# Writing out the hardware loops of two expert stages, with 23 expert numbers held in registers

## The reference, cut to what matters

```python
def ffn(x, w_gate, b_gate, W1, b1, W2, b2):         # x: 2048 x 128
    probs = softmax(x @ w_gate + b_gate)            # 8 experts
    route_p, route_idx = max(probs), argmax(probs)
    h = relu(x @ W1[e] + b1[e])                     # 128 -> 512, for each expert e
    y = h @ W2[e] + b2[e]                           # 512 -> 128
    return y[route_idx] * route_p
x = x + 0.5 * ffn(layernorm(x))
x = x + attention(layernorm(x))
x = x + 0.5 * ffn(layernorm(x))
```

## Time and profile before

| | |
|---|---|
| median of 3 runs | 393.47 us (392.41 to 393.94) |
| span of the profiled execution, first to last instruction | 387.9 us |
| TensorE busy | 270.7 us, 70% of the span |
| VectorE busy | 228.1 us, 59% |
| GpSimd busy | 204.0 us, 53% |
| ScalarE busy | 135.8 us, 35% |
| mean granted TensorE clock | 0.867 of full speed |

### The profile page before, as it was taken

One profiled execution on the slowest core, in us unless ns is written; L12 is line 12 of the kernel. 1 busy time (PEld: TensorE's weight loads), 2 busy tenths in 40 slices (PEclk: granted clock), 3 DMA queues, 4 the chain that ended last, 5 costly groups with the idle time before them and its releaser, 6 DMA issues.

```text
span 387.9 us, 7595 instructions
## 1 busy us (share of the span) xinstructions
PE 270.7 (70%) x2114; PEld 199.2 (51%) x2115; DVE 228.1 (59%) x609; ACT 135.8 (35%) x319; POOL 204.0 (53%) x351
## 2 busy tenths in 40 slices
PE   0641487777943865798999999999770396777760
PEld 0540476776831433344555555554560296777760
DVE  4959344343529778756677676776628444444434
ACT  2400132222311444056667566667420032322220
POOL 2922756666535564156565565656612566666550
PEclk9999999888985769579999999999865588968995
DMA  7950111112222055575122121100200111111217
GB/s 215 417 166 0 41 36 50 42 42 41 41 73 63 2 162 167 175 224 162 54 58 69 46 70 54 55 30 1 83 27 0 28 43 47 44 41 37 46 35 216
DMA packets 34203, 31.06 MB, mean 80 GB/s; under 512 B 3265, under 2 KB 28226, under 8 KB 34178
## 3 DMA queue, kind: packets, MB, share of 16 engines
q1 hardware_dynamic: 31234, 24.72, 20.4%
q0 software_dynamic: 2944, 6.04, 6.1%
HBM read 18.09 MB, written 12.45 MB: 79 GB/s over the span
## 4 chain that ended last, share of the span: by engine, by line
PE 57%; DVE 15%; DMA 8%; SPq 6%; issue 6%; POOL 4%; ACT 2%; another core or an unknown queue 1%; DVEq 0%; POOLq 0%; ACTq 0%
PE bank L1048 13%; PE bank L1059 13%; PE bank L1159 4%; PE bank L1185 4%; SPq L350 4%; PE bank L1135 3%; DVE xn L709 3%; DVE x L856 3%; PE bank L1182 3%; PE bank L1201 2%; PE bank L1165 2%; DVE hot_lane L787 2%; DMA xs_sb<-xn_d,tok_g 2%; DMA qz<-mT 2%; PE bank L1040 2%
## 5 line engine op out<-in xcount | busy, mean ns | idle before, releaser
L636 ACT ACTIVATE pT<-bank 128x512 f32<-128x512 f32 x96 | 57.4, 599 | 41.7 <-PE bank L1159 20.7
L439 POOL DMA_INDIRECT y_d<-ys_sb,tok_s x46 | 46.7, 1014 | 39.8 <-DVE ys_sb L831 33.2
L1059 PE MATMUL bank<-experts,hT 128*128 x368 | 56.1, 301 | 15.3 <-ACT hT L573 6.7
L1048 PE MATMUL bank<-xsT,ew 128*128 128x128 f32 x368 | 57.9, 309 | 8.6 <-ACT xsT L567 7.8
L1059 PEld LDWEIGHTS bank<-experts,hT 128*128 128x128 f32 x368 | 50.6, 213 | 17.6 <-issue 17.5
L1048 PEld LDWEIGHTS bank<-xsT,ew 128*128 128x128 f32 x368 | 53.2, 222 | 10.8 <-ACT xsT L567 8.8
L433 POOL DMA_INDIRECT xs_sb<-xn_d,tok_g x46 | 45.2, 982 | 20.3 <-issue 12.5
L902 DVE TENSOR_REDUCE mh<-bank 128x2 f32<-128x512 f32 x64 | 44.0, 689 | 13.9 <-PE bank L1135 13.3
L573 ACT ACTIVATE hT<-bank,ew 128x128 f32<-128x128 f32 x92 | 29.0, 368 | 58.2 <-PE bank L1048 46.0
L813 DVE TENSOR_SCALAR hT<-bank,ew 128x128 f32<-128x128 f32 x92 | 27.9, 345 | 36.2 <-PE bank L1048 27.2
L516 POOL TENSOR_SCALAR_AFFINE_SELECT pT<-pT 128x512 f32<-128x512 f32 x64 | 40.9, 639 | 0.0
(11 more groups left out here) (125 smaller groups left out, 429.4 us busy)
## 6 DMA issues: line engine op xcount, KB each, us to landing
sp_d<-spl SPq DMA_DIRECT2D x32, 192.0 KB, 2.9
experts<-in_experts SPq DMA_DIRECT2D x8, 578.0 KB, 8.8
qz<-sp_d SPq DMA_DIRECT2D x32, 96.0 KB
ks<-sp_d SPq DMA_DIRECT2D x32, 96.0 KB
xn_d<-xn SPq DMA_DIRECT2D x8, 256.0 KB, 3.1
yg<-y_d SPq DMA_DIRECT2D x8, 256.0 KB, 3.7
x<-in_x SPq DMA_DIRECT2D x4, 256.0 KB, 4.5
out<-x SPq DMA_DIRECT2D x4, 256.0 KB, 2.4
```

The source lines that it names most:

```text
L439: pool.indirect_dma_start(y_d[:, :], bass.IndirectOffsetOnAxis(ap=tok_s[:, t:t + 1], axis=0), ys_sb[:, t % OUT, :], None).then_inc(e_st[f] ...
L636: act.activation(pT[:, u, :], bank[2 + u % 2][:, :], ACT.Exp, scale=SCALE).then_inc(a_e, 1)
L1048: mm = pe.matmul(bank[2 + 2 * (k % 2) + c // 2][:, (c % 2) * P:(c % 2 + 1) * P], ew[:, k % WRING, c * P:(c + 1) * P], xsT[:, k % 2, :], st ...
L1059: mm = pe.matmul(bank[6 + k % 2][:, 0:D], hT[:, k % 2, c, :], w2.rearrange("p a c -> p (a c)"), start=(c == 0), stop=(c == HC - 1))
```

## The change

On ScalarE, VectorE and TensorE the loop over tiles 6 to 17 goes, and all 23 tiles are written out. On VectorE and TensorE the expert numbers are no longer read tile by tile. At the head of its stage each of these two engines waits for `te` and reads all 23 numbers into 23 registers; `weights` and `output` use the registers. VectorE's wait for `te` was at the head of its stage already, TensorE's is new. GpSimd's and SyncE's lists stay as they are. The part on ScalarE is the same replacement of the loop without the registers.

```diff
             def expert_tiles(f):                      # VectorE
+                dve.wait_ge(r_te[f], 1)
+                tile_expert = [dve.value_load(te[0:1, t:t + 1], min_val=0, max_val=NE - 1) for t in range(NS)]
+
                 def weights(t, k):
-                    e = dve.value_load(te[0:1, bass.ds(t, 1)], min_val=0, max_val=NE - 1)
+                    e = tile_expert[t]
                     need(dve, e_yc[f], t - WRING + 1)
...
-                dve.wait_ge(r_te[f], 1)
                 dve.wait_ge(e_all, 16 * NE)
                 for t in range(WRING):
                     weights(t, t)
                 relu(0, 0, 0)
-                for k in range(RING):
-                    step(k, 0, k)
-                with dve.Fori(1, NS // RING) as i:
-                    for k in range(RING):
-                        step(RING * i + k, i, k)
-                for t in range(NS // RING * RING, NS):
-                    step(t, NS // RING, t % RING, do_w=t + WRING < NS, do_h=t + 1 < NS)
+                for t in range(NS):
+                    step(t, t // RING, t % RING, do_w=t + WRING < NS, do_h=t + 1 < NS)
...
             def expert_tiles(f):                      # TensorE
+                pe.wait_ge(r_te[f], 1)
+                tile_expert = [pe.value_load(te[0:1, t:t + 1], min_val=0, max_val=NE - 1) for t in range(NS)]
...
                 def output(t, k):
-                    e = pe.value_load(te[0:1, bass.ds(t, 1)], min_val=0, max_val=NE - 1)
+                    e = tile_expert[t]
...
-                for k in range(RING):
-                    step(k, 0, k)
-                with pe.Fori(1, NS // RING) as i:
-                    for k in range(RING):
-                        step(RING * i + k, i, k)
-                for t in range(NS // RING * RING, NS):
-                    step(t, NS // RING, t % RING, do_T=t + 2 < NS, do_h=t + 1 < NS)
+                for t in range(NS):
+                    step(t, t // RING, t % RING, do_T=t + 2 < NS, do_h=t + 1 < NS)
```

More of the change, by code:

```diff
@@ L584, in expert_tiles @@
                 relu(0, 0, 0)
-                for k in range(RING):
-                    step(k, k)
-                with act.Fori(1, NS // RING) as i:
-                    for k in range(RING):
-                        step(RING * i + k, k)
-                for t in range(NS // RING * RING, NS):
+                for t in range(NS):
                     step(t, t % RING, do_T=t + 2 < NS, do_h=t + 1 < NS)
```

## The result

The changed kernel takes 405.07 us (median of four runs, 401.23 to 409.69) against 393.71 us (four runs, 392.41 to 397.26) beside it: a ratio of 1.0255 with a 95% interval of 1.0155 to 1.0354. The forecast was 410.5 us, range 399 to 417. The span of the profiled execution is 399.4 us, 11.5 us above that of before, where 17 was forecast. The two stages together are 17.1 us longer in this pair of profiles, as forecast; 5 us ahead of them that have nothing to do with the change hide part of it.

A forecast was written before the change was run, and what follows sets the result against it. No engine was full; GpSimd was nearest to a bound, 50.5 us without a pause in the first stage's 61.8 us. Span 387.9 + 20.0 (reads) - 3 (steps) = 404.9 us; time 393.47 + 17.0 = 410.5 us, range 399 to 417 us.

The forecast's parts named there:

- The reads at the head: Head of both expert stages: 23 reads in a row delay the first hidden product, 20.0 us together.
- cheap reads: Rival at the stage heads: reads overlap at a 0.30 us pitch, kernel takes 396.4 us; chance 0.12.
- TensorE's head "beside VectorE's": Stage head: TensorE's 23 reads run beside VectorE's, end 1 us earlier and cost nothing; without VectorE's, nearly as much.
- GpSimd can't work ahead: GpSimd's queue at the stage head: seven gathers at most during the reads, its remaining 50 us start 10 us later.
- What comes back in the steps: Tile steps of both stages: fewer reads and no loop give 3 us back, bounds 0 and about 23 us.
- The loop's part: Loop over tiles 6 to 17: its branches and additions cost 0 to 3 us in both stages.
- The sum: Whole kernel: 387.9 + 20.0 - 3 = 404.9 us of span, 393.47 + 17.0 = 410.5 us of time.
- The runs' median stands 5.6 us above the profiled span: Whole kernel: offset between profiled span and median time, used to turn 404.9 us into 410.5 us.
- Loop edges: Rival in the tile loop: stalls on entering a pass, 8.4 us, go; 402.1 us; chance 0.12, shared with half the pauses.
- Its other half: Rival in the tile steps: quicker steps bring back half of GpSimd's pauses, 11.5 us; 402.0 us; shared chance 0.12.
- GpSimd without pauses: Rival in both stages: all 23.1 us of GpSimd's pauses come back, kernel takes 390.4 us; chance 0.06.

The follow-up runs named there:

- Experiment 4: The changed kernel with the 23 reads at the head of both engines made without the bounds check; 398.55 us, ratio 1.017 to the kernel before.
- experiment 2: The changed kernel with the 23 head reads on TensorE alone, VectorE reading ahead of each weight copy again; 405.03 us, ratio 1.034 to the kernel before.
- experiment 1: The kernel before with all 23 tiles written out, each expert number still read tile by tile; 392.28 us against 391.97 us, ratio 0.992.
- experiment 3: The changed kernel with the head reads on VectorE alone, TensorE reading in each output product again; 407.63 us, ratio 1.042 to the kernel before.
- 7: Tiles written out, no head reads, VectorE reading for tile t + 3 at its step's start; 389.23 us against 392.64 us for the kernel before.
- 9: The kernel before with tiles written out, VectorE's reads one step ahead and GpSimd's clears held back; 384.40 us against 393.37 us, ratio 0.981.
- experiment 6: The changed kernel with GpSimd's clears at the front held back until VectorE has scaled the attention weights; 404.06 us, ratio 1.038 to the kernel before.
- Experiment 8: The changed kernel with VectorE making three reads, its first three weight copies, then the other 20 reads; 404.69 us (one run).
- experiments 5: The kernel before with GpSimd's clears at the front held back until VectorE has scaled the attention weights; 388.21 us against 392.64 us, ratio 0.994.

## Why the prediction was right, step by step

**The reads at the head** are right in kind and size. Forecast were 0.62 us a read on VectorE and 0.65 us on TensorE, delays of 10.3 and 9.7 us. Measured are 0.61 us (from the second read on) and 0.66 us, and delays of 10.3 and 9.5 us. The cheap reads are refuted by the chain: load, operations and check follow each other without overlap. Experiment 4 shows the parts one by one, 0.35 us of load and 0.26 us of check.

**TensorE's head "beside VectorE's"** was put at nothing, with a margin of 1 us. Measured: it ends 0.6 us before VectorE's first copy starts (48.43 and 49.02 us), and alone it costs all but 0.4 to 0.5 us of the whole (experiment 2). That was foreseen with "would cost nearly as much". The margin was even thinner than the 1 us, so that it held is in part luck.

**GpSimd can't work ahead**: right. Its timeline has the two new pauses of 7.0 and 4.9 us, and gather 6 is all that lies between them. Counted as in the prediction (from scatter 0 to the end of the last one, less the queue's work and 11.4 us of gaps), its pauses are 8.7 and 8.5 us in place of 11.3 and 11.8, within the 8 to 11 us forecast.

**What comes back in the steps** was forecast as 3 us in both stages, bounds 0 and 23. Measured between first and last scatter: 61.6 us before and 59.3 us changed (means of four stretches each), so 4.5 us come back. The loop's part of it is near nothing (experiment 1: 61.9 us). That leaves the steps without a read, and the size fits, but it isn't shown: with only VectorE's reads gone from the steps (experiment 3) the mean is 60.5 us, with them moved one step ahead (7 and 9) 60.7 us, and in experiment 6, the same stages as the changed kernel, 60.5 us in place of 59.3. Experiment 8, with the same steps once more, has 59.7 us. The term lies within the spread of equal stages (59.0 to 61.1 us over the changed kernel, 6 and 8).

**The sum.** The change was forecast at 17.0 us; the first pair of profiles has 17.1 us in the two stages (8.5 and 8.6), the means of the table have 15.9, and experiments 5 and 6 differ by 15.9 us in their medians. That the spans of the first comparison differ by 11.5 us has one reason: ahead of the first gather the changed kernel's profile is 5.1 us shorter, because of the clears; that leaves 12.0 us, and 0.5 us are won outside of the stages. Which of its two spans the forecast of 404.9 us was held against was chance: it is 5.5 us above the first (399.4) and 0.9 us below the later one (405.8). The 11.4 us between the median times are explained only in part. The changed kernel's median lies between its two pairs of runs, and of the kernel before the runs spread over 386.9 to 398.3 us in all comparisons together, for reasons that the profiles don't show: both of its profiles have the long copies, at 388 and 389 us of span.

The level has an error of its own. I added 5.6 us between span and time to the sum. In every run that has both numbers the time is 1.7 to 1.8 us above the span (401.23 and 399.4, 407.58 and 405.8, 390.49 and 388.7), so the profiled execution of before belongs to a time of about 389.7 us (an estimate, since its own time isn't on record) and was itself a quick one, below the three that I compared it with. The step of the forecast that this concerns is "The runs' median stands 5.6 us above the profiled span": 387.9 + 1.8 + 17.0 = 406.7 us would have been nearer to the 405.07 us.

**The rivals.** Cheap reads (396.4 us) would have needed a pitch of 0.30 us. Loop edges (402.1 us) look near by the time alone; experiment 1 shows stretches as long as before without the loop, and the pieces of "issue" that the rival rested on are in the changed kernel too. Its other half, 11.5 us of pauses brought back, would need some 56 us between first and last scatter (61.6 less half of 11.5); it is 59.3 us. GpSimd without pauses didn't come: in the changed kernel it still waits 16.4 us for out copies in the first stage, as in the earlier trace rows, here its group from the first scatter on:

```profile
L439 POOL DMA_INDIRECT y_d<-ys_sb,tok_s x23 | 24.5, 1065 | 20.1 <-DVE ys_sb L827 16.4 <-issue 3.7
```

4.9 us of these are the wait ahead of scatter 0, where before it was 2.0 us.

**What stays open.** Why experiments 4 and 5 have longer stretches between the scatters; when a copy gets in between two clears and when not; and what makes the long pauses. Where they begin the traces do show. From one timeline of the kernel before, over all engines:

```profile
59.51 1.06 PE L1048 MATMUL bank<-xsT,ew 128*128 128x128 f32 x8
...
63.86 0.63 ACT L573 ACTIVATE hT<-bank,ew 128x128 f32<-128x128 f32 x2 [3.36 <-PE bank L1048]
...
64.83 1.15 PE L1059 MATMUL bank<-experts,hT 128*128 x8 [2.15 <-issue]
```

The hidden product ends at 60.57 us by the profile, yet its ReLU starts at 63.86 us on both engines, and the 2.15 us of "issue" are TensorE waiting for that ReLU. In all 13 profiles, with and without loops and with the reads in any place, 3 to 6 of the 23 tiles of a stage have a ReLU on ScalarE that starts 1 to 4.8 us after both the end of its product and ScalarE's own last instruction; none of the last three tiles, which have no gathers beside them, has. The ends of matmuls are modelled in the profile, so it can't tell a late end from a late signal. Neither the loop nor a read in the step is needed for it.

## What to carry to other kernels

Work on a sequencer costs nothing where it fills a wait and everything where it stands ahead of the first instruction of a stage: 23 reads of 0.6 us for each engine and stage, spread over the tiles, cost too little to be told from the spread (4.5 us at most over both stages, loops included), and the same reads in a row cost 10 us a stage, on either engine. If a value must come early, read it one step ahead, and look which engine's list is the next in line before moving one of two equal heads. Before a loop is written out for its speed, compare the pitch inside and outside of it in the same trace. And subtract profiles stretch by stage, not span from span: here 5.1 us, against 17.1 us in the stages, lay in a part that the change doesn't touch.

## What the runs showed of the hardware

A clear on GpSimd and a copy on VectorE, with nothing in common but the time at which they run, can hold each other up. Two `tensor_scalar` of 128x128 with SBUF on both sides take 0.60 us alone (experiments 5, 6 and 9), and 8.78 or 3.53 us beside clears of 128x2048, seemingly until the end of the last clear or of one in between. Where they got in early, the next `tensor_scalar` (128x384) took 2.04 us in place of 0.41 to 0.44, and two of the clears took 1.95 and 2.01 us in place of 1.80. Reductions and `tensor_tensor` beside the same clears keep their 0.2 to 0.3 us. The Trainium skill, "VectorE: DVE Perf Modes", section "Two Vector instructions with no wait between them", says that an instruction in a two-port mode reads through a second SBUF interface that it shares with GpSimd. The traces fit it as far as they show `tensor_scalar`, and not others, being held; they don't show in which mode an instruction runs, and the clears have no input to read.

A load from SBUF into a sequencer's register took 0.30 us, the first of a row 0.49 to 0.55 us. In a row the loads came every 0.35 us (VectorE) or 0.37 us (TensorE) without a bounds check and every 0.61 us (VectorE) or 0.66 us (TensorE) with one, and nothing of two reads overlapped.
